# Half the drives of four sequences made by ScalarE and turned back by TensorE, and a rearranged head, in a fused scan and expert kernel

## The chip, the cores and the metric

One core of one Trainium2 chip runs the kernel. The metric is the device time of one execution in microseconds, and lower is better. The profile of one execution gives its span, from the first to the last instruction, and beside it that execution's own device time, which is a little longer than the span.

## What is computed

Eight sequences of 512 rows by 128 channels go through a selective state scan and then a mixture of experts (top 2 of 8). Cut to what matters here:

```python
xn = layernorm(layernorm(x)) * gamma + beta
dt = softplus(xn @ W_dt.T + b_dt)            # [T, D]
B, C = xn @ W_B.T, xn @ W_C.T                # [T, 16]
for n in range(16):                          # per state, per channel d
    h[t] = exp(-dt[t]*exp(A_log[d, n])) * h[t-1] + dt[t] * xn[t, d] * B[t, n]
    y[t] += C[t, n] * h[t]
x1 = x + layernorm(y + D * layernorm(x))
x2 = layernorm(x1);  gates = softmax(x2 @ gate_w + gate_b);  top 2 experts
out = x1 + layernorm(sum_k gate_k * (relu(x2 @ w1[e_k] + b1[e_k]) @ w2[e_k] + b2[e_k]))
```

All is float32. The product `dt * xn * B` is called the drive of a state, `exp(-dt*...)` its decay.

## The kernel before

In the scan part channels lie on partitions and time runs along the free dimension. Each sequence has 16 states, worked on in 8 pairs (`n` counts pairs over all sequences, `h` is the half). For one state VectorE makes the drive (`drive`, L915: `b_rep * gx_ps`, where `b_rep` is a row of B spread over all partitions by a DMA and `gx_ps = dt*xn` lies in PSUM) and then runs the scan (`scan`, L924). ScalarE makes the decay (`decay_`, L793). GpSimd multiplies both states of a pair with the spread C (`weigh`, L662), and TensorE sums them into `y_ps` by transposes (`reduce`, L1170). Two PSUM banks `u_ps[0]`, `u_ps[1]` hold the drives of the two halves (NU = 2), `hs` holds three pairs (NH = 3), and the decays have five buffers (NA = 5).

Ahead of each sequence's scans, ScalarE normalises (`norm`, L745), TensorE turns (L1136), ScalarE applies gamma and beta (`channels`, L767), TensorE makes B and C (`states`, L1151), ScalarE copies them (`rows`, L773) for a trip through DRAM, TensorE makes the logits of dt (`delta`, L1155), ScalarE makes the two halves of the softplus (L779 to L784), GpSimd adds them (`dt_add`, L653), and VectorE makes `gx_ps` (L904). All of these PSUM products share one bank, `misc`.

After every two sequences (a group) VectorE makes the routing, GpSimd scatters the 8 x 128 rows of the group twice by 16 indirect DMAs (L680) into expert slots in DRAM, and 23 tiles of 128 slots each go through `tile_turn`, `tile_up` (L1252, into `hid_ps`), `tile_relu` (ScalarE, L841, into `hid_t`), and `tile_down` (L1264). 92 tiles in all. The first banks and buffers of the tiles, `hid_ps` and `hid_t`, are idle until the first tile. At the end rows are gathered (L692), mixed on VectorE and stored.

Every engine works through one fixed list in order. The list is made in `planned()`, which plays the steps through a model: COST holds a modelled duration for each kind, `at(urgency, kind, ...)` names what a step waits for, and among the steps that are ready on an engine the smallest urgency number goes first. Where TensorE would idle, the planner puts a filler (`warm`, L1228), a bf16 matmul of zeros. SP alone issues the loads and stores, GpSimd the indirect ones.

The head of the program (before the list begins) loads sequence 0 and ten small parameters on SP, makes the statistics of sequence 0 on VectorE, waits on ScalarE for all ten small loads, exponentiates A_log there, waits for VectorE's sign change, and normalises sequence 0 on ScalarE.

## Time and profile before

| what | value |
|---|---|
| median of 3 runs | 479.35 us (477.76 to 479.82) |
| the profiled execution's own time | 477.24 us |
| its span | 475.5 us |
| busy of the span | PE 411.9 us (87%), DVE 354.3 (75%), ACT 317.7 (67%), POOL 297.5 (63%) |
| mean granted TensorE clock | 0.939 |

PE is TensorE (PEld its weight loads), DVE VectorE, ACT ScalarE, POOL GpSimd, SP SyncE. A busy PE in the scan part is to a large part fillers. The list of costliest groups is read by line; a stage table gives each engine's busy time within a stretch, which tells better than a share of the whole span which engine is full there.

### The profile page before, as it was taken

The numbers are of one execution on the slowest core, as the hardware profiler recorded it, in microseconds if no ns is written. First come the engines' busy times: TensorE is split into PE (matmuls) and PEld (weight loads), VectorE is DVE, ScalarE is ACT, GpSimd is POOL, SyncE is SP. The second block draws the span as 40 slices with busy tenths as digits, with TensorE's granted clock in tenths as the row PEclk, the third lists the DMA queues.
The fourth block names the chain that finished last, engine by engine and source line by source line (L and its number), as shares of the span: only waits on it lengthen the run. The fifth ranks groups of instructions, "written<-read, shape, count | busy, mean of one in ns | idle before, by whom it ended". The sixth has DMA issues, their size and how long they took to land.

```text
span 475.5 us, 9846 instructions
## 1 busy us (share of the span) xinstructions
PE 411.9 (87%) x2847; PEld 324.4 (68%) x2869; DVE 354.3 (75%) x834; ACT 317.7 (67%) x830; POOL 297.5 (63%) x219
## 2 busy tenths in 40 slices
PE   4459999998799989998989996699899999899950
PEld 1136566464456547897886796699799999899840
DVE  4699999999999999999999999596335524000355
ACT  3678584681377378779988867385775977667723
POOL 1157566481699946358995459578777770777720
PEclk8569999999899999999999999799999999899965
DMA  5699988896798878999899999984698788766341
GB/s 141 216 424 355 331 326 312 297 305 224 215 355 298 318 228 294 331 324 367 287 410 353 340 305 219 364 287 116 179 271 234 210 246 216 203 198 183 97 133 45
DMA packets 78147, 125.50 MB, mean 264 GB/s; under 512 B 7832, under 2 KB 50592, under 8 KB 74000
## 3 DMA queue, kind: packets, MB, share of 16 engines
q1 hardware_dynamic: 73776, 116.01, 75.2%
q0 software_dynamic: 4320, 8.86, 6.0%
q8 instruction: 26, 0.43, 0.4%
q14 instruction: 25, 0.20, 0.1%
HBM read 105.95 MB, written 18.89 MB: 263 GB/s over the span
## 4 chain that ended last, share of the span: by engine, by line
PE 30%; DVE 14%; DMA 8%; issue 7%; POOL 5%; ACT 5%; SPq 0%; DVEq 0%; ACTq 0%; POOLq 0%
PE out_ps L1264 10%; PE hid_ps L1252 7%; DMA w_tile<-w_rows 5%; DVE hs L924 4%; DVE u_ps L915 3%; POOL slots_in L680 3%; PE y_ps L1170 3%; ACT hid_t L841 3%; PE u_ps L1252 2%; DMA slots_in<-x,pos 2%; PE misc L1222 2%; POOL ch L662 1%; DMA xt<-slots_in 1%; ACT mix L860 1%; PE y_ps L1228 1%
## 5 line engine op out<-in xcount | busy, mean ns | idle before, releaser
L662 POOL TENSOR_TENSOR ch<-hs,c_rep 128x1024 f32<-128x1024 f32 x64 | 151.1, 2364 | 72.2 <-DVE hs L924 65.0
L924 DVE TENSOR_TENSOR_SCAN hs<-ab,u_ps 128x512 f32<-128x512 f32 x128 | 150.4, 1203 | 0.1
L793 ACT ACTIVATE ab<-dt,decay 128x512 f32<-128x512 f32 x128 | 89.3, 718 | 48.7 <-DVE hs L924 48.4
L1264 PE MATMUL out_ps<-w_f,hid_t 128*128 x736 | 102.8, 284 | 6.8 <-ACT hid_t L841 3.3
L1264 PEld LDWEIGHTS out_ps<-w_f,hid_t 128*128 128x128 f32 x736 | 91.6, 195 | 13.7 <-issue 12.0
L841 ACT ACTIVATE hid_t<-hid_ps,w_tile 128x128 f32<-128x128 f32 x244 | 69.2, 375 | 27.8 <-PE hid_ps L1252 20.0
L1228 PE MATMUL y_ps<-none 128*128 128x512 bf16 x351 | 85.9, 382 | 0.8
L915 DVE TENSOR_TENSOR u_ps<-b_rep,gx_ps 128x512 f32<-128x512 f32 x128 | 81.9, 678 | 0.2 <-issue 0.2
L680 POOL DMA_INDIRECT slots_in<-x,pos x64 | 64.7, 1012 | 25.8 <-issue 13.9
L1252 PE MATMUL hid_ps<-xt_t,w_tile 128*128 128x128 f32 x488 | 66.3, 280 | 9.1 <-DMA w_tile<-w_rows 6.5
L1170 PE MATMUL y_ps<-ident,ch 128*128 128x128 f32 x512 | 67.6, 277 | 5.8 <-POOL ch L662 5.8
L1170 PEld LDWEIGHTS y_ps<-ident,ch 128*128 128x128 f32 x512 | 59.2, 143 | 14.3 <-POOL ch L662 10.5
L1252 PEld LDWEIGHTS hid_ps<-xt_t,w_tile 128*128 128x128 f32 x488 | 60.3, 194 | 12.1 <-DMA w_tile<-w_rows 6.9
L1228 PEld LDWEIGHTS y_ps<-none 128*128 128x128 bf16 x371 | 36.4, 100 | 36.3 <-issue 3.3
L692 POOL DMA_INDIRECT c_rep<-slots_out,pos x32 | 31.7, 991 | 20.7 <-PE out_ps L1264 12.3
L1049 DVE SCALAR_TENSOR_TENSOR mix<-c_rep,weight,misc 128x128 f32<-128x128 f32 x24 | 6.7, 343 | 36.1 <-PE misc L1214 36.1
L841 ACT ACTIVATE hid_t<-u_ps,w_tile 128x128 f32<-128x128 f32 x84 | 24.0, 373 | 8.1 <-PE u_ps L1252 8.1
L850 ACT ACTIVATE ot<-out_ps 128x256 f32<-128x256 f32 (+1 forms) x48 | 18.3, 382 | 13.8 <-PE out_ps L1264 13.7
L703 POOL DMA_INDIRECT yg_dram<-ot,dst x23 | 22.7, 989 | 7.3 <-issue 7.3
L653 POOL TENSOR_TENSOR dt<-sp_l,sp_r 128x512 f32<-128x512 f32 x8 | 10.2, 1275 | 23.2 <-ACT sp_l L784 23.2
L1252 PE MATMUL u_ps<-xt_t,w_tile 128*128 128x128 f32 x168 | 22.4, 277 | 0.1
L1228 PE MATMUL out_ps<-none 128*128 128x512 bf16 x76 | 20.8, 408 | 1.3 <-DVE zeros L1095 1.3
(134 smaller groups left out, 482.1 us busy)
## 6 DMA issues: line engine op xcount, KB each, us to landing
b_rep<-rows_dram SPq DMA_DIRECT2D x64, 512.0 KB, 6.6
c_rep<-rows_dram SPq DMA_DIRECT2D x32, 1024.0 KB, 8.0
w_tile<-w_rows SPq DMA_DIRECT2D x92, 258.0 KB, 4.2
slots_in<-zeros SPq DMA_DIRECT2D x3, 1472.0 KB, 9.9
slots_out<-ot SPq DMA_DIRECT2D x33, 128.0 KB
xt<-slots_in SPq DMA_DIRECT2D x15, 256.0 KB
x<-x SPq DMA_DIRECT2D x8, 256.0 KB, 4.8
out<-mix SPq DMA_DIRECT2D x8, 256.0 KB, 2.5
```

Source lines behind the costliest of these rows:

```text
L662: nc.gpsimd.tensor_tensor(ch[:, n % NCH], hs[:, n % NH], c_rep[:, r // 2, 2 * (r % 2):2 * (r % 2) + 2].rearrange("p n t -> p (n t)"), ALU. ...
L680: nc.gpsimd.indirect_dma_start(out=slots_in[g], out_offset=bass.IndirectOffsetOnAxis(pos[:, r // K, K * b + r % K:K * b + r % K + 1], 0), ...
L692: nc.gpsimd.indirect_dma_start(out=yg(b)[:, r, :], out_offset=None, in_=slots_out[g], in_offset=bass.IndirectOffsetOnAxis(pos[:, r // K, K ...
L703: nc.gpsimd.indirect_dma_start(out=yg_dram, out_offset=bass.IndirectOffsetOnAxis(dst[:, i:i + 1], 0), in_=ot[:, m % NO, j * D:(j + 1) * D] ...
L793: nc.scalar.activation(ab[:, i % NA], dt[:, b % 2], ACT.Exp, scale=decay[:, 2 * r + h:2 * r + h + 1]).then_inc(s["decayed"], 1)
L841: last = nc.scalar.activation(hid_t[:, q % NHT, c * P:(c + 1) * P], hidden(q)[:, c * P:(c + 1) * P], ACT.Relu, bias=w_tile[:, q % NW, HID ...
L915: nc.vector.tensor_tensor(u_ps[i % NU][:], b_rep[:, n % NBR, h], gx_ps[:], ALU.mult).then_inc(s["driven"], 1)
L924: nc.vector.tensor_tensor_scan(hs[:, n % NH, h * T:(h + 1) * T], ab[:, i % NA], u_ps[i % NU][:], 0.0, ALU.mult, ALU.add).then_inc(s["scann ...
L1170: last = nc.tensor.matmul(y_ps[:, k * P:(k + 1) * P], ch[:, n % NCH, h * T + k * P:h * T + (k + 1) * P], ident[:], start=False, stop=(r == ...
L1228: nc.tensor.matmul(y_ps[:] if y_open else out_ps[:], none[:], none[:, 0:1].to_broadcast([P, T]), start=not y_open, stop=not y_open)
L1252: last = nc.tensor.matmul(hidden(q)[:, c * P:(c + 1) * P], w_tile[:, q % NW, c * P:(c + 1) * P], xt_t[:, m % NB, j * P:(j + 1) * P], start ...
L1264: last = nc.tensor.matmul(out_ps[:, j * D:(j + 1) * D], hid_t[:, q % NHT, c * P:(c + 1) * P], w2_f[:, bass.ds(e * HC * D + c * D, D)], sta ...
```

## The change

In sequences 0 to 3, in pairs 1 to 7 of each, the second half's drive (28 drives in all) is no longer made on VectorE from a spread row of B. Instead: once a sequence, TensorE makes B with time on partitions (`b_cols`, 4 small matmuls) and ScalarE copies it (`b_copy`); GpSimd makes a second `dt*xn` in SBUF (`gx_copy`); TensorE turns it into `hid_ps[1]` (`gx_turn`, 4 transposes). Once a drive, ScalarE multiplies the turned rows by the column of B as a per-partition scale, in four instructions of 128 x 128 (`weigh_gx`, into one of the three `hid_t` buffers), and TensorE turns the result back into `u_ps[1]` by 4 transposes (`u_turn`). For these pairs `b_spread` loads one row, not two. The tiles wait for the last `u_turn`, since they use the same buffers.

In the head, the parameters needed early come on two queues (two weights first on SP, five others on ScalarE's queue), the remaining three are loaded after the sequences; sequence 0 is normalised on VectorE, its delta goes to `hid_ps[0]` without waiting for the copy of the rows, and the sum of its softplus is made on VectorE right before `gx`. The fillers ahead of the first turn are 14, not 10, and two follow it; the planner places fillers from 16.0 us of its model, not 12.0, and starts each engine at a given time. Nearly all urgencies have new values, so that the lists of all engines are in another order to the end.

```diff
@@ constants and the planner @@
+TURNED_SEQS = 4
+TURNED = [b * PAIRS + r for b in range(TURNED_SEQS) for r in range(1, PAIRS)]
+TURN_NO = {n: j for j, n in enumerate(TURNED)}
+NSC = 3
-WARM, WARM_UP, HEAD_WARM = 0.26, 12.0, 10
+WARM, WARM_UP, HEAD_WARM, TURN_WARM = 0.26, 16.0, 14, 2
+BUSY_UNTIL = {"DVE": 6.1, "ACT": 6.4, "PE": 7.0, "POOL": 2.7, "SP": 8.5}
...
-    at(9.5, "weights_2", 0, 0, scan_of(2 * PAIRS))
+    at(1.5, "weights_2", 0, 0, scan_of(2 * PAIRS))
...
-        at(2.5, "stats", b, 0)
+        at(7.5, "stats", b, 0)
...
-        at(0, "gx", b, 0, ("dt_add", b, 0), ("drive", n0 - 1, 1))
+        at(12, "gx", b, 0, dt_of(b), last_drive(n0 - 1))
+        if b < TURNED_SEQS:
+            at(1.5, "b_cols", b, 0, ("channels", b, 0))
+            at(3.5, "b_copy", b, 0, ("b_cols", b, 0), ("weigh_gx", n0 - 1, 1))
+            at(14, "gx_copy", b, 0, dt_of(b), ("gx_turn", b - 1, 0))
+            at(2.5, "gx_turn", b, 0, ("gx_copy", b, 0), ("weigh_gx", n0 - 1, 1))
...
-            at(20, "spread", b, q, ("rows_out", b, 0), ("weigh", n0 - PAIRS + 2 * q + 1, 0))
+            at(10.5, "spread", b, q, ("rows_out", b, 0), ("weigh", n0 - PAIRS + 2 * q + 1, 0))
...
-                at(16.5, "drive", n, h, ("b_spread", n, 0), ("gx", b, 0), ("scan", *before(n, h, NU)))
+                if h and n in TURN_NO:
+                    j = TURN_NO[n]
+                    at(6.5, "weigh_gx", n, h, ("gx_turn", b, 0), ("b_copy", b, 0), *([("u_turn", TURNED[j - NSC], 1)] if j >= NSC else []))
+                    at(4.5, "u_turn", n, h, ("weigh_gx", n, 1), ("scan", *before(n, h, NU)))
+                else:
+                    at(21, "drive", n, h, ("b_spread", n, 0), ("gx", b, 0), ("scan", *before(n, h, NU)))
...
-            at(11.5, "weigh", n, 0, ("scan", n, 1), ("spread", b, n % PAIRS // 2), ("reduce", n - NCH, 0))
-            at(2, "reduce", n, 0, ("weigh", n, 0), ("skip_copy", b, 0), ("x1", b - 1, 0))
+            at(10, "weigh", n, 0, ("scan", n, 1), ("spread", b, n % PAIRS // 2), ("reduce", n - NCH, 0))
+            at(0.5, "reduce", n, 0, ("weigh", n, 0), ("skip_copy", b, 0), ("x1", b - 1, 0))
...
-                at(2, "scatter", b, r, ("slots", g, 0), ("clear", g, 0), *([("id_shift", b, 0)] if g == SENT and r >= K else []))
+                at(9, "scatter", b, r, ("slots", g, 0), ("clear", g, 0), *([("id_shift", b, 0)] if g == SENT and r >= K else []))
...
-            at(9, "tile_weights", q, 0, ("slots", g, 0), ("tile_relu", q - NW, 0))
+            at(0, "tile_weights", q, 0, ("slots", g, 0), ("tile_relu", q - NW, 0))
@@ SP @@
-                             rows_dram[b % 2][2 * r:2 * r + 2, :].rearrange("n t -> (n t)")[None, :]
-                             .to_broadcast([P, 2 * T])).then_inc(b_loaded[n % NBR], 16)
+                             rows_dram[b % 2][2 * r:2 * r + m, :].rearrange("n t -> (n t)")[None, :]
+                             .to_broadcast([P, m * T])).then_inc(b_loaded[n % NBR], 16)
...
+            for dst, src in ((w_bc[:], w_bc_t), (w_dt[:], w_dt_t)):
+                sp.dma_start(dst, src).then_inc(s["small_w"], 16)
@@ GpSimd @@
+            def gx_copy(b, _):
+
+                pool.wait_ge(s["dt_ready"], b + 1)
+                after(pool, s["gx_turned"], b)
+                nc.gpsimd.tensor_tensor(gx_s[:], dt[:, b % 2], xa[:, b % 2], ALU.mult).then_inc(s["gx_copied"], 1)
@@ ScalarE @@
+            def weigh_gx(n, h):
+
+                b, r = n // PAIRS, n % PAIRS
+                j = TURN_NO[n]
+                act.wait_ge(s["gx_turned"], b + 1)
+                act.wait_ge(s["b_copied"], b + 1)
+                after(act, s["u_turned"], j - NSC + 1)
+                for k in range(K):
+                    last = nc.scalar.activation(hid_t[:, j % NSC, k * P:(k + 1) * P], hid_ps[1][:, k * P:(k + 1) * P], ACT.Identity,
+                                                scale=b_t[:, k, 2 * r + h:2 * r + h + 1])
+                last.then_inc(s["u_weighed"], 1)
...
+            for dst, src in ((gam[:], gamma[:, None]), (bet[:], beta[:, None]), (decay[:], a_log), (bdt[:], b_dt[:, None]),
+                             (skip[:], d_param[:, None])):
+                act.dma_start(dst, src).then_inc(s["small_a"], 16)
             act.wait_ge(s["dve_set"], 1)
             scales(0, 1, 1)
-            act.wait_ge(s["small"], 16 * 10)
+            act.wait_ge(s["small_a"], 16 * 5)
@@ VectorE @@
             def gx(b, _):
 
+                if b == 0:
+                    dve.wait_ge(s["sp_log"], 1)
+                    nc.vector.tensor_tensor(dt[:, 0], sp_l[:], sp_r[:], ALU.add).then_inc(s["dt_ready"], 1)
                 dve.wait_ge(s["dt_ready"], b + 1)
...
-                dve.wait_ge(s["driven"], i + 1)
+                if h and n in TURN_NO:
+                    dve.wait_ge(s["u_turned"], TURN_NO[n] + 1)
+                else:
+                    dve.wait_ge(s["driven"], drives(n, h))
...
+            for k in range(K):
+                last = nc.vector.tensor_scalar(xn[:, 0, k], x1[:, k], rs[:, 1, 0, k:k + 1], nb_x[:, 1, 0, k:k + 1], ALU.mult, ALU.add)
+            last.then_inc(s["normed"], 1)
@@ TensorE @@
+            def b_cols(b, _):
+
+                pe.wait_ge(s["xa_ready"], b + 1)
+                misc_free("b_cols", b + 1)
+                for k in range(K):
+                    last = nc.tensor.matmul(misc[:, k * N:(k + 1) * N], xa[:, b % 2, k * P:(k + 1) * P], w_bc[:, 0:N], start=True,
+                                            stop=True)
+                last.then_inc(s["b_cols"], 1)
+
...
+            def u_turn(n, h):
+
+                j, i = TURN_NO[n], 2 * n + h
+                pe.wait_ge(s["u_weighed"], j + 1)
+                after(pe, s["scanned"], i - NU + 1)
+                for k in range(K):
+                    last = nc.tensor.matmul(u_ps[i % NU][:, k * P:(k + 1) * P], hid_t[:, j % NSC, k * P:(k + 1) * P], ident[:],
+                                            start=True, stop=True, is_transpose=True)
+                last.then_inc(s["u_turned"], 1)
```

## Rows read from the trace of the kernel before

**Rows 1.** The page: busy time of each engine, and 40 slices of the span.

```profile
PE 411.9 (87%) x2847; PEld 324.4 (68%) x2869; DVE 354.3 (75%) x834; ACT 317.7 (67%) x830; POOL 297.5 (63%) x219
...
DVE  4699999999999999999999999596335524000355
...
PEclk8569999999899999999999999799999999899965
```

**Rows 2.** Busy time by stage: from:to, length, then busy us of each engine.

```profile
21.30:48.90 27.60, 21.16 (x111) 13.44 (x114) 27.27 (x35) 21.02 (x40) 17.46 (x9) 0.80 0.99 389
48.90:81.70 32.80, 32.54 (x186) 19.40 (x187) 31.80 (x58) 21.34 (x40) 20.05 (x10) 1.00 0.91 319
81.70:126.50 44.80, 40.71 (x223) 22.76 (x226) 43.48 (x93) 23.15 (x44) 22.14 (x13) 1.00 0.78 263
126.50:160.50 34.00, 32.43 (x176) 19.54 (x180) 33.75 (x56) 21.45 (x41) 31.38 (x22) 0.95 0.95 326
...
390.00:455.00 65.00, 60.46 (x487) 56.97 (x487) 11.73 (x50) 43.93 (x147) 41.26 (x42) 0.97 0.64 176
```

**Rows 3.** Costliest groups: line, tiles, count, busy us and mean ns, idle before.

```profile
L662 POOL TENSOR_TENSOR ch<-hs,c_rep 128x1024 f32<-128x1024 f32 x64 | 151.1, 2364 | 72.2 <-DVE hs L924 65.0
L924 DVE TENSOR_TENSOR_SCAN hs<-ab,u_ps 128x512 f32<-128x512 f32 x128 | 150.4, 1203 | 0.1
...
L915 DVE TENSOR_TENSOR u_ps<-b_rep,gx_ps 128x512 f32<-128x512 f32 x128 | 81.9, 678 | 0.2 <-issue 0.2
...
L653 POOL TENSOR_TENSOR dt<-sp_l,sp_r 128x512 f32<-128x512 f32 x8 | 10.2, 1275 | 23.2 <-ACT sp_l L784 23.2
```

**Rows 4.** Timeline of VectorE in sequence 2: start us, duration us.

```profile
97.38 1.27 DVE L915 TENSOR_TENSOR u_ps<-b_rep,gx_ps 128x512 f32<-128x512 f32 x2
98.55 2.33 DVE L924 TENSOR_TENSOR_SCAN hs<-ab,u_ps 128x512 f32<-128x512 f32 x2
```

**Rows 5.** Timeline of the head, ScalarE and VectorE.

```profile
5.92 0.23 DVE L896 SCALAR_TENSOR_TENSOR nb_x<-mv,rs 128x4 f32<-128x4 f32 x2 [0.95 <-ACT rs L737]
...
8.46 0.21 ACT L868 ACTIVATE decay<-decay 128x16 f32<-128x16 f32 x1 [2.57 <-DMA gate_bias<-gate_b]
...
9.42 0.87 DVE L881 BATCH_NORM_STATS2 st<-x 128x6 f32<-128x128 f32 x4
...
17.35 0.38 DVE L885 BATCH_NORM_AGGREGATE mv<-st 128x2 f32<-128x6 f32 x4
21.34 0.70 DVE L904 TENSOR_TENSOR gx_ps<-dt,xa 128x512 f32<-128x512 f32 x1 [3.61 <-POOL dt L653]
...
23.73 2.32 DVE L924 TENSOR_TENSOR_SCAN hs<-ab,u_ps 128x512 f32<-128x512 f32 x2
```

**Rows 6.** Timeline of ScalarE: four 128-wide instructions from PSUM, and from SBUF.

```profile
284.29 1.15 ACT L841 ACTIVATE hid_t<-hid_ps,w_tile 128x128 f32<-128x128 f32 x4 [0.59 <-PE hid_ps L1252]
285.31 1.35 ACT L793 ACTIVATE ab<-dt,decay 128x512 f32<-128x512 f32 x2
```

```profile
8.92 1.65 ACT L745 ACTIVATE xn<-x,nb_x,rs 128x128 f32<-128x128 f32 x4 [0.24 <-DVE decay L1102]
```

**Rows 7.** TensorE: its granted clock by stretch (busy, then PEclk), and its timeline.

```profile
8.00:24.00 16.00, 6.16 (x12) 0.51 0.77 242
...
36.00:60.00 24.00, 23.75 (x138) 1.00 0.99 340
```

```profile
41.31 0.60 PE L1144 MATMUL misc<-ident,xu 128*128 128x128 f32 x4
...
42.39 1.03 PE L1170 MATMUL y_ps<-ident,ch 128*128 128x128 f32 x8
```

```profile
127.71 1.90 PE L1170 MATMUL y_ps<-ident,ch 128*128 128x128 f32 x8 [2.95 <-POOL ch L662]
```

**Rows 8.** The last scatter of group 0, and a stall of the tile stage.

```profile
162.86 1.27 POOL L680 DMA_INDIRECT slots_in<-x,pos  x1 [0.17 <-issue]
```

```profile
300.95 2.07 PE L1252 MATMUL hid_ps<-xt_t,w_tile 128*128 128x128 f32 x8 [5.68 <-DMA w_tile<-w_rows]
```

More of the change, by code:

```diff
@@ L104 @@
 HOP = 0.18
[L105 removed]
+WARM, WARM_UP, HEAD_WARM, TURN_WARM = 0.26, 16.0, 14, 2
+BUSY_UNTIL = {"DVE": 6.1, "ACT": 6.4, "PE": 7.0, "POOL": 2.7, "SP": 8.5}
 ROW_DMA, ROW_GAP = ("scatter", "gather", "tile_send"), 1.3
 ON = {
[L108 to L109 removed]
+    "DVE": "norm_first dt_first stats shift_all gx drive scan y_stats x1 x1_shift gate_bias gate_max softmax second starts slots mix mix_shift add tile_ids id_shift",
+    "ACT": "scales_all norm norm_u skip_copy channels rows softplus decay y_scale x1_scale x2 weigh_gx b_copy gate_copy gate_exp weigh_copy "
            "mix_scale result tile_copy tile_relu tile_keep",
[L111 to L112 removed]
+    "PE": "turn turn_u states b_cols gx_turn u_turn delta delta_first reduce gate_turn gate_logits count weigh_turn bias_mix tile_turn tile_pick tile_up tile_down",
+    "POOL": "gx_copy dt_add weigh scatter gather tile_send",
     "SP": "weights_2 clear rows_out b_spread spread tile_weights tile_load tile_store yg_load store",
@@ L149, in tasks @@
[L149 to L154 removed]
+        if b:
+            at(11, "norm", b, 0, ("shift_all", 0, 0), due)
+        else:
+            at(5, "norm_first", 0, 0)
@@ L510, in hidden, with drives @@
             return free[(q - alone) % len(free)]
+        def drives(n, h):
+            return 2 * n + h + 1 - sum(m < n or m == n and h == 1 for m in TURNED)
         def walk(parts):
@@ L1272, in _ @@
             turn_x(0, 0)
-            pe.wait_ge(s["small"], 16 * 10)
-            walk(dict(turn=lambda b, r: turn_x(b, r) if b else None, turn_u=turn_u, states=states, delta=delta, reduce=reduce,
+            for i in range(TURN_WARM):
+                warm(i, 0)
+            pe.wait_ge(s["small_w"], 16 * 2)
+            walk(dict(turn=lambda b, r: turn_x(b, r) if b else None, delta_first=delta, turn_u=turn_u, states=states, b_cols=b_cols, gx_turn=gx_turn, u_turn=u_turn, delta=delta, reduce=reduce,
                       gate_turn=gate_turn, gate_logits=gate_logits, count=count, weigh_turn=weigh_turn, bias_mix=bias_mix,
```

220 lines of the change are left out of this document (125 added, 95 removed).

## The prediction

> **What bounds the kernel now.** I read the page's slices first, then a table of busy time by stage, then the groups, and last the timelines of the head and of two spots. The slices [rows 1] show VectorE at nine tenths or more from the third slice to the twenty-fifth, so from about 24 to 297 us, while TensorE's 87% of busy time is partly fillers there. The stage table [rows 2] cuts the part that the change touches into the four sequences 0 to 3, from one `gx` to the next: 27.6 + 32.8 + 44.8 + 34.0 = 139.2 us, in which VectorE is busy 27.27 + 31.80 + 43.48 + 33.75 = 136.3 us (98%), ScalarE 87.0 and GpSimd 91.0. So VectorE sets the pace there, and nothing but its own list does. In the last of the four GpSimd is nearly as full, 31.38 of 34.0 us, since the 16 scatters of group 0 lie between its products. Behind the scans it is TensorE: 60.5 of 65 us busy in 390 to 455 [rows 2], with tiles, not fillers.
>
> **The drives taken from VectorE.** A drive lasts 678 ns and a scan 1203 ns in the groups [rows 3], but they overlap a little when queued. Two drives start at 97.38 and what follows starts at 98.55 [rows 4], so a drive costs 1.17 / 2 = 0.59 us of VectorE's time. 28 x 0.59 = 16.5 us leave it, 4.1 a sequence. That is the most the turned drives can give: 119.8 us of work in place of 136.3.
>
> **What ScalarE gets.** A turned drive is four 128-wide instructions that read PSUM with a per-partition operand. The nearest row is the tiles' relu, also four from PSUM: start 284.29, next instruction 285.31, so 1.02 us [rows 6]. The other bound is the normalisation, four from SBUF with two such operands, 1.65 us [rows 6]. I take 1.02, because the source is PSUM. The Trainium skill ("VectorE: DVE Perf Modes", section on the errata of SBUF sources) gives ScalarE 172 cycles plus one an element for PSUM and 224 for SBUF, at 1.2 GHz; an estimate by it is 4 x 0.25 = 1.0 us, and no run here shows the cause of the difference. Seven a sequence and one copy of B (at most the 0.26 us of one of the four): 7.4 us, or 11.8 at the other bound. Over four sequences ScalarE goes from 87.0 to 116.6 us, against VectorE's 119.8. By stage it is tighter. Some of its busy time is overlap that closes when it is full (a lone decay shows 0.72, a queued one 1.35 / 2 = 0.68, and the second of the relu group starts every 0.26 us while each lasts 0.38), some 1.5 us a sequence:
> - sequence 0: VectorE 27.27 - 4.1 = 23.2, ScalarE 21.0 + 7.4 - 1.5 = 26.9, of 27.6: ScalarE bounds, gain 0.7, with the fifth of it that it can put off to the next, 1.0.
> - sequence 1: VectorE 27.7, ScalarE 27.2, of 32.8: both full in lists that wait on each other, so 1 us above the larger and 0.5 for what was put off: gain 3.6.
> - sequence 2 has group 0's routing on VectorE: 39.4 against ScalarE 29.1, of 44.8: gain 4.1, the whole of it.
> - sequence 3: VectorE 29.6, ScalarE 27.4, GpSimd 31.4 + 1.3 for `gx_copy` (priced as the other 128x512 sum, 1275 ns [rows 3]) = 32.7, of 34.0. GpSimd bounds, but `hs` lets it lag three pairs into sequence 4: gain 2.0.
> Sum 10.7 us of the 16.5. The low bound is ScalarE at 1.65 us a drive: 11.8 + 21.3 - 1.5 = 31.6 us in each of sequences 0, 1 and 3, that is 0 (or 4 lost in sequence 0), 1 and 2 gained, 4 in sequence 2: some 3 us in all. The high bound is 16.5.
>
> **What TensorE gets.** 28 `u_turn`, 4 `gx_turn`, 4 `b_cols`, each four instructions: a turn of four is 0.60 us at the full clock [rows 7], so 21.6 us, in place of fillers, which fill far more than that. Price nothing while the fillers are the cover. On the path there is a deadline: `u_turn` of a pair can start only when the scan before it has freed `u_ps[1]`, and VectorE reaches the scan that needs it after one drive and one scan, 0.59 + 1.12 = 1.71 us. 0.60 us and two hops fit. Behind a `reduce` of 1.03 us [rows 7] it is 1.63 plus the hops, about late. Queued behind a late `u_turn` on VectorE are that scan, the next drives and through them GpSimd's product.
>
> **What leaves the DMA queues.** 28 rows less of B, 256 KB each: 7 MB. No engine waits for them: VectorE idled 0.2 us in all in front of its drives [rows 3]. So nothing.
>
> **The head.** Before, `nb_x` is there at 6.15, but ScalarE waits until 8.46 for the last of ten small loads, passes through the sign change, and normalises at 8.92 for 1.65 us [rows 5, 6]; TensorE's clock has then fallen to 1.2 GHz (0.51 granted from 8 to 24 us [rows 7]). `gx` starts at 21.34, the first scan at 23.73. After, the chain (normalise on VectorE at 6.2, turn 0.6, channels 0.8, states and delta 1.0 each at 2.4 GHz, softplus 2.6, hops) is done by about 14.3. But the sum for dt is written inside `gx`, and in the planner's list `gx` comes after the seven statistics (urgency 7.5 against 12). So VectorE's own list sets it: 6.15 + 1.1 to normalise (bounds 0.5 and 1.65) + 0.9 of small casts + the seven statistics, 17.73 - 9.42 = 8.3 us [rows 5] = 16.4; dt sum 0.7, `gx` 0.7, shift 0.3 (a broadcast row of B, asked for at about 12, must have landed by then), two drives 1.2: the first scan at 19.3, so 4.4 us earlier. Bounds: 3 us, if the five loads issued by ScalarE delay it or `gx` and GpSimd's `gx_copy` get in each other's way, and 6.5, if the statistics are spread out.
>
> **What follows.** From 160.5 us on the change removes nothing; it only comes earlier. Group 0's last scatter is at 162.86 [rows 8], so the tiles begin after the turned sequences in any case, and their wait for the last `u_turn` costs nothing. Tiles, scans, routing and mixing all hang on the scans before them, and TensorE has no free stretch behind them that would hold back the gain. So the whole 10.7 + 4.4 = 15.1 us arrives at the end. The new order from there on I price at nothing, bounds 5 us to both sides: before, it has a stall of 5.7 us for expert weights at 295 to 301 [rows 8], which could go or come twice. 477.24 - 15.1 = 462.1 against the profiled execution's own time; the median of the runs is 2.1 us above that, so 462 to 464, and I say 463.
>
> **Rivals.**
> - Full gain: ScalarE's work is spread well by the new urgencies, 16.5 + 4.4, perhaps with the stall gone: 451 to 456. For it: over four sequences all three engines fit below 120 us. Against: in-order lists, and sequence 0.
> - ScalarE is the bound: 1.3 us or more a drive, or its list stops in front of `weigh_gx` and holds the decays. Gain 3 + 4.4 down to 3: 470 to 476. For it: 26.9 of 27.6 us already at the low price.
> - The clock falls: in the turned sequences float32 transposes take the place of bf16 fillers. At 1.2 GHz a `reduce` is 1.90 us [rows 7] and a turn 1.1; 8 x 1.9 + 7 x 1.1 + some 9 us of the rest = 32 us a sequence, so TensorE would bound at 32 and only 4.4 + 5 remain: 468 to 470. Against: from 36 to 60 us such transposes stand among fillers and the clock granted is 1.00 [rows 7], and most fillers stay. The Trainium skill ("TensorE: Matmul & The Clock Gate", section on transposes) says that a transpose does not count as busy for the clock; by that rule this is the way it goes.
> - Slower: the turned drive comes late. One mechanism: `u_turn` stands behind a `reduce` in TensorE's list, which itself waits for GpSimd's product, and the scan behind it waits. If that is 1.3 us for each of the 28 (cold `reduce` 1.90 and turn 1.1 against the 1.71 there are), 36 us are lost: 477 - 15 + 36 = 498. It decides from 15.1 / 28 = 0.54 us a drive; at 1 us a drive the time is 490.
> - The drives leave, but nothing gains: head only and a worse order behind, 477 to 481.
>
> **Numbers.** Forecast 0.50 (456 to 469), full gain 0.17, ScalarE bound 0.12, clock 0.06, nothing 0.05, slower 0.10. A difference under 0.5%, 2.4 us, is what a measurement of this kernel cannot tell from none. Faster are the first four, 0.85; same 0.05; slower 0.10. The range 452 to 475 leaves out the slower cases, the edge of no gain and the best end.
>
> **What would show it.** In the stage table after, from one `gx` to the next: VectorE 4 us less busy in each of the four, ScalarE 7 more, at 95% or more in sequences 0 and 1. First scan at about 19.3, the statistics still in front of `gx`. Four `weigh_gx` instructions at 1.0 us. `gx` of sequence 4 at about 145.4 where it was at 160.5. VectorE's scans waiting for `u_turn` under 5 us in all. Wrong would be: VectorE idle for more than 15 us in that part, a granted clock under 0.9 from 40 to 140 us, or a tile stage longer than before by as much as the scans gained.

## The result and the profile after

The kernel after takes 486.15 us (median of 4 runs, 485.24 to 488.15), the kernel before beside it on the same chip 479.59 us: ratio 1.0151, 95% interval 1.0109 to 1.0192. The change makes the kernel 1.5% slower, where 463.0 us had been forecast. The profiled execution took 485.79 us, its span is 484.1 us.

The page of the kernel after, busy time and slices, against [rows 1]:

```profile
PE 423.4 (87%) x2964; PEld 341.1 (70%) x2991; DVE 351.8 (73%) x811; ACT 344.4 (71%) x942; POOL 302.0 (62%) x222
...
DVE  6878989999998999999999899487334534000255
...
PEclk9799999999899999999998979799999999999965
```

ScalarE has 27 us more work, as it should. VectorE has 2.5 us less, where 28 drives less at 678 ns each come to 19 us in the sum of durations, and the head's new work on it (normalisation and the dt sum) to 1.8 us more. So something gave VectorE time back. The mean granted clock is 0.947, before 0.939.

The stage table, the same four stretches as in [rows 2], from `gx` to `gx`, and sequence 4 and the tiles (length, then busy time of PE, PEld, DVE, ACT, POOL, granted clock):

```profile
17.38:48.30 30.92, 30.36 (x171) 19.02 (x174) 25.43 (x29) 25.61 (x65) 19.54 (x10) 0.91 0.60 218
48.30:82.50 34.20, 31.29 (x199) 21.13 (x202) 30.94 (x50) 28.16 (x70) 21.75 (x11) 1.00 0.67 241
82.50:129.80 47.30, 40.21 (x228) 25.42 (x231) 44.94 (x83) 33.34 (x85) 23.78 (x12) 0.93 0.79 277
129.80:160.30 30.50, 30.01 (x185) 19.39 (x187) 28.36 (x50) 26.20 (x61) 27.75 (x20) 1.00 0.82 283
160.30:204.30 44.00, 41.16 (x280) 30.23 (x283) 42.81 (x84) 29.19 (x68) 28.05 (x15) 1.00 0.88 294
390.00:455.00 65.00, 62.53 (x516) 58.52 (x516) 13.73 (x62) 45.49 (x152) 38.63 (x40) 1.00 0.71 194
```

The head is 4 us shorter, about as forecast: `gx` of sequence 0 starts at 17.38, not 21.34. But the four turned sequences take 142.9 us in place of 139.2, so `gx` of sequence 4 comes at 160.3, where it came before (160.5), and not at 145.4. In the new list 62 scans stand ahead of that `gx`, before 63, so for like work (a scan is 1.1 us) the part is nearer 4.8 us longer. VectorE's busy time in them went from 136.3 to 129.7 us, not to 119.8, and its idle time from 2.9 to 13.2. ScalarE is nowhere near full (25.6 of 30.9), and neither is GpSimd, which in sequence 3 is at 27.75 of 30.5. Behind sequence 4's `gx`, where no code changed, the kernel after takes 484.1 - 160.3 = 323.8 us against 315.0 before: 8.8 us more, of which 7.7 are in the scans (they end at 337.3, before at 329.8). So the result splits in three: head -4.0, turned part +3.7, behind it +8.8, together +8.5, where the spans differ by 8.6.

What VectorE waits for in the turned part, as the waits of the trace list them (us in total, times, longest):

```profile
DVE hs L998 <- PE u_ps L1264: 5.8, 9, 1.3
DVE nb_x L963 <- ACT rs L778: 1.5, 1, 1.5
DVE gx_ps L975 <- POOL dt L688: 1.3, 2, 0.7
DVE hs L998 <- issue: 0.5, 1, 0.5
```

That is 9 of the 13.2 us of idle time; the others are short gaps, such as the 0.09 us between the end of a lone drive and its scan. The rest of the loss hides inside instructions. The timeline of VectorE at a pair with one drive, and at `gx` of sequence 1, then GpSimd at that place:

```profile
75.58 0.67 DVE L986 TENSOR_TENSOR u_ps<-b_rep,gx_ps 128x512 f32<-128x512 f32 x1
76.34 2.42 DVE L998 TENSOR_TENSOR_SCAN hs<-ab,u_ps 128x512 f32<-128x512 f32 x2
78.67 0.68 DVE L986 TENSOR_TENSOR u_ps<-b_rep,gx_ps 128x512 f32<-128x512 f32 x1
...
48.30 2.83 DVE L975 TENSOR_TENSOR gx_ps<-dt,xa 128x512 f32<-128x512 f32 x1 [0.66 <-POOL dt L688]
```

```profile
48.22 2.35 POOL L703 TENSOR_TENSOR ch<-hs,c_rep 128x1024 f32<-128x1024 f32 x1
50.53 1.72 POOL L694 TENSOR_TENSOR gx_s<-dt,xa 128x512 f32<-128x512 f32 x1
```

Two things are to be read here. First, the pair lasts 78.67 - 75.58 = 3.09 us (3.01 to 3.10 in the others that wait for nothing). In the kernel before, a pair with two drives starts at 97.38 [rows 4], and the next row of that timeline is

```profile
100.79 1.27 DVE L915 TENSOR_TENSOR u_ps<-b_rep,gx_ps 128x512 f32<-128x512 f32 x2
```

so that pair lasts 3.41 us (3.42 in most). The first scan starts 0.76 us after the lone drive, where two drives together took 1.17: the scan reads what the drive before it has just written, and nothing stands between them. So a drive that leaves is worth 1.17 - 0.76 = 0.41 us, and 0.33 to 0.41 by the whole pair, not 0.59. Second, `gx` lasts 2.83 us where [rows 5] has 0.70. It isn't shown as waiting, but it ends 0.56 us after GpSimd's product does (48.22 + 2.35 = 50.57; 48.30 + 2.83 = 51.13), and `gx_copy`, which GpSimd starts at 50.53, takes 1.72 us in place of 1.27. Both engines seem to take turns.

### The profile page after: what moved, and what is told of

Same layout as the page of the kernel before. It is cut to its first block, busy times and chain, and to the rows that moved or that the text cites. A ratio compares the mean times of both kernels' runs of the same rounds, so it can differ in the third digit from the quotient of the medians.

```text
span 484.1 us, 10253 instructions
## 1 busy us (share of the span) xinstructions
PE 423.4 (87%) x2964; PEld 341.1 (70%) x2991; DVE 351.8 (73%) x811; ACT 344.4 (71%) x942; POOL 302.0 (62%) x222
## 4 chain that ended last, share of the span: by engine, by line
PE 31%; DMA 8%; issue 7%; POOL 5%; ACT 4%; DVE 4%; SPq 1%; POOLq 0%; ACTq 0%; DVEq 0%
PE out_ps L1377 11%; PE hid_ps L1365 7%; PE u_ps L1365 3%; DMA w_tile<-w_rows 2%; PE misc L1335 2%; ACT hid_t L906 2%; PE y_ps L1281 2%; PE gx_ps L1365 2%; POOL ch L703 1%; DMA slots_out<-ot 1%; POOL slots_in L721 1%; DMA slots_in<-x,pos 1%; PE misc L1327 1%; DMA rows_dram<-rows 1%; POOL yg_dram L744 1%
## 5 line engine op out<-in xcount | busy, mean ns | idle before, releaser
L1377 PEld LDWEIGHTS out_ps<-w_f,hid_t 128*128 128x128 f32 x736 | 91.2, 195 | 14.5 <-issue 13.0
L1365 PE MATMUL hid_ps<-xt_t,w_tile 128*128 128x128 f32 x488 | 69.0, 287 | 6.7 <-issue 5.3
L1341 PE MATMUL y_ps<-none 128*128 128x512 bf16 x268 | 70.0, 385 | 1.1 <-issue 0.2
L1365 PEld LDWEIGHTS hid_ps<-xt_t,w_tile 128*128 128x128 f32 x488 | 62.9, 201 | 8.7 <-issue 8.3
L986 DVE TENSOR_TENSOR u_ps<-b_rep,gx_ps 128x512 f32<-128x512 f32 x100 | 65.0, 680 | 0.6 <-issue 0.3
L1341 PEld LDWEIGHTS y_ps<-none 128*128 128x128 bf16 x292 | 29.0, 100 | 25.4 <-issue 4.2
L843 ACT ACTIVATE hid_t<-hid_ps,b_t 128x128 f32<-128x128 f32 x112 | 31.4, 386 | 5.5 <-PE hid_ps L1254 3.4
L1341 PE MATMUL out_ps<-none 128*128 128x512 bf16 x116 | 32.2, 422 | 1.4 <-DVE zeros L1171 1.3
L906 ACT ACTIVATE hid_t<-u_ps,w_tile 128x128 f32<-128x128 f32 x84 | 24.0, 372 | 11.4 <-PE u_ps L1365 11.2
L733 POOL DMA_INDIRECT yg_first<-slots_out,pos x16 | 15.4, 962 | 14.2 <-DMA slots_out<-ot 9.9
L1341 PEld LDWEIGHTS out_ps<-none 128*128 128x128 bf16 x119 | 12.6, 107 | 15.8 <-issue 6.0
```

The source lines that it names most:

```text
L733: nc.gpsimd.indirect_dma_start(out=yg(b)[:, r, :], out_offset=None, in_=slots_out[g], in_offset=bass.IndirectOffsetOnAxis(pos[:, r // K, K ...
L843: last = nc.scalar.activation(hid_t[:, j % NSC, k * P:(k + 1) * P], hid_ps[1][:, k * P:(k + 1) * P], ACT.Identity, scale=b_t[:, k, 2 * r + ...
L906: last = nc.scalar.activation(hid_t[:, q % NHT, c * P:(c + 1) * P], hidden(q)[:, c * P:(c + 1) * P], ACT.Relu, bias=w_tile[:, q % NW, HID ...
L986: nc.vector.tensor_tensor(u_ps[i % NU][:], b_rep[:, n % NBR, h], gx_ps[:], ALU.mult).then_inc(s["driven"], 1)
L1341: nc.tensor.matmul(y_ps[:] if y_open else out_ps[:], none[:], none[:, 0:1].to_broadcast([P, T]), start=not y_open, stop=not y_open)
L1365: last = nc.tensor.matmul(hidden(q)[:, c * P:(c + 1) * P], w_tile[:, q % NW, c * P:(c + 1) * P], xt_t[:, m % NB, j * P:(j + 1) * P], start ...
```

## The experiments

The kernels up to undo_same_list ran on chips on which the kernel before itself takes 503 to 505 us, the others where it takes 479; each ratio is to the kernel before on the same chip. On a slower chip the kernel before has `gx` of sequence 4 at 160.9, as on the other (160.5), and its whole surplus lies behind the scans. So the times up to there can be read across both.

### Head, turned drives and new lists apart

**head_old_order**, **all_old_order** and **new_order_no_turn** let the planner make new lists, with the urgencies of before for the first two.

```diff
# head_old_order: the kernel after with
-TURNED_SEQS = 4
+TURNED_SEQS = 0
-        todo[kind, i, part] = (urgency,
+        todo[kind, i, part] = (OLD.get(kind, urgency),      # the urgencies of before
# all_old_order: the second edit alone; new_order_no_turn: the first alone
```

> The head of the change and all its other code, no turned sequence, and the urgencies of the kernel before. Both theories (A: the new order of the lists costs the time; B: the turned drives themselves cost it) expect the 4.0 us that gx came earlier in the changed kernel: 475.6 against a before of 479.6. If it is 478 or more, the 4 us of the head are given back later whatever the drives do.

> The whole change, but with the urgencies of the kernel before (new kinds keep theirs, norm_first, delta_first and dt_first take those of norm, delta and dt_add). Theory A (the new order costs the time): 462 to 470, gx of sequence 4 at 150 or earlier. Theory B (the turned drives cost it): 476 to 482, gx of sequence 4 near 160 as in the changed kernel.

> The changed kernel with no turned sequence, new urgencies and new head. Theory A: 482 to 488, as slow as the changed kernel or slower. Theory B: 472 to 477, the head's gain and nothing else.

Measured: 1.0316 (1.0239 to 1.0392), 1.0846 (1.0772 to 1.0919) and 1.0034 (0.999 to 1.0078). Old urgencies fit neither the new head (`gx` of sequence 0 at 26.1 us, later than before) nor the turned work (`gx` of sequence 4 at 176.2). Lists planned from urgencies that were chosen for another graph cost 3% with the new head alone, and 8% with the turned drives in them. So a kernel that is planned anew measures its lists first and its edit second.

new_order_no_turn fell between its two theories. It has `gx` of sequence 0 at 17.4, `gx` of sequence 4 at 158.2 and the end of the scans at 332.2. Two things follow. The new urgencies lose 5.3 us between `gx` of sequence 4 and the end of the scans (174.1 against 168.8 in before_again) with no turned drive in the kernel. And the kernel after is slower than the same urgencies without turned drives: 1.0151, and 1.0192 on a slower chip, against 1.0034 there. With the lists planned anew for each, the turned drives cost over 1%.

**drop28** leaves the 28 drives out of the kernel before and plans anew; the scans of these pairs read a product that is left over in their bank, so the output is another one.

> The kernel before with 28 drives left out (second halves of pairs 1 to 7 in sequences 0 to 3; their scans run over what the bank held, so the output is wrong), nothing in their place. It is the most that VectorE can be given. If a drive is worth 0.59 us, as predicted: 479.6 - 16.5 = 463. If the first drive's result is exposed once no second drive stands behind it (a pair took 3.02 to 3.09 us in the changed kernel, against 3.42), 28 x 0.37 = 10 us: 469. If the gain is lost behind the scans: 475 or more.

It took 1.0289 (1.0224 to 1.0354): less work on the fullest engine, and 2.9% slower. Its one profile (of an execution of 524.67 us, the median is 518.35) shows where: `gx` of sequence 4 comes at 152.9, so the four sequences take 131.6 us in place of 139.2, 1.1 us of it a scan that stands behind that `gx` here. Behind it all is lost again, since the scans end at 344.5 where they ended at 329.8, and VectorE waits there 7.4 us for `y_ps` and 7.0 us for `rs_y` from ScalarE. In other lists, then, a good half of the freed time does arrive at the end of this part. From here on lists were held fixed.

**before_again** and **after_again** are both kernels as they are.

> The kernel before, unchanged, for a trace on the chip of this call: the first four runs fell on a chip where it took 505 us, not 479. Both theories expect the ratio 1.00 to itself. It is to show in which stage and on which engine a chip's 25 us lie (if DMA: landing times up and waits for w_tile; if an engine: its mean durations up).

> The changed kernel, unchanged, beside the others of this call. If the 1.5% are the same on every chip: ratio 1.010 to 1.020. If they depend on how a fixed list meets a chip's transfer times, the ratio can be anything from 0.98 to 1.05.

The kernel before showed a span of 507.4 us there in its one profiled execution; the kernel after has ratio 1.0192 (1.0124 to 1.0261), in line with the first chip.

### The drives, with the lists held

**drop28_same_list** keeps every list of the kernel before and only skips 28 drives. **undo_same_list** keeps every list of the kernel after and puts the drives back on VectorE, each as early as its bank allows, with no turned work.

```diff
# drop28_same_list: the kernel before with
+DROP = [(8 * b + r, 1) for b in range(4) for r in range(1, 8)]
             def drive(n, h):
+                if (n, h) in DROP:
+                    return
# undo_same_list: the kernel after with
-b_cols=b_cols, gx_turn=gx_turn, u_turn=u_turn, b_copy=b_copy, weigh_gx=weigh_gx, gx_copy=gx_copy,
+# drive(m, 1) is issued right after drive(m, 0) and scan(m - 1, 1)
```

> The kernel before with the 28 drives left out (their scans run over what the bank held, so the output is wrong) and every list otherwise exactly as before; the first time the planner had made new lists for it, and it was 2.9% slower. Theory A (new lists cost the time, and a drive less is a drive less): ratio 0.965 to 0.98, that is 10 to 16 us less, from 0.37 to 0.59 us a drive. Theory B (VectorE's time in sequences 0 to 3 is not what the end hangs on): ratio 0.99 to 1.00.

> The changed kernel with its lists as they are, but the 28 drives back on VectorE, each behind the first drive of its pair, and nothing of the turned work issued (weigh_gx, u_turn, gx_copy, gx_turn, b_cols, b_copy), two rows of B loaded. Theory A (order): 3 to 10 us slower than the changed kernel, since VectorE gets 28 drives back in unchanged lists. Theory B (the turned work costs what it gives): within 3 us of the changed kernel or faster than it.

drop28_same_list: 0.9972 (0.9931 to 1.0013). From `gx` to `gx` over four sequences it takes 140.8 us, before 139.2 (139.4 on this chip), though 11.4 us of work left VectorE. This run breaks the forecast's main step, in the lists of before, without any turned work in it. Its VectorE groups in this stretch (busy and mean ns of one; the fifth `gx` is that of sequence 4), and the timelines of VectorE and of GpSimd around one of the small shifts of a normalisation:

```profile
L909 DVE TENSOR_TENSOR gx_ps<-dt,xa 128x512 f32<-128x512 f32 x5 | 10.7, 2131 | 3.6 <-POOL dt L658 3.6
L953 DVE SCALAR_TENSOR_TENSOR nb<-mv,rs 128x4 f32<-128x4 f32 x3 | 7.3, 2426 | 0.3 <-ACT rs L732 0.2
L942 DVE SCALAR_TENSOR_TENSOR shift<-mv_y,rs_y 128x4 f32<-128x4 f32 x3 | 2.8, 924 | 0.3 <-ACT rs_y L732 0.3
```

```profile
145.49 0.67 DVE L922 TENSOR_TENSOR u_ps<-b_rep,gx_ps 128x512 f32<-128x512 f32 x1
146.08 2.67 DVE L953 SCALAR_TENSOR_TENSOR nb<-mv,rs 128x4 f32<-128x4 f32 x1
148.67 1.21 DVE L931 TENSOR_TENSOR_SCAN hs<-ab,u_ps 128x512 f32<-128x512 f32 x1
```

```profile
145.36 0.98 POOL L685 DMA_INDIRECT slots_in<-x,pos  x1 [0.17 <-issue]
146.37 2.35 POOL L667 TENSOR_TENSOR ch<-hs,c_rep 128x1024 f32<-128x1024 f32 x1
```

An instruction on four columns takes 2.67 us and ends as GpSimd's product ends (148.75 and 148.72). In this part of this run all the lines that stretch so read two tensors from SBUF: `gx`, `nb`, `shift`, and in the routing `r_sub` and `run` (elsewhere `eq` and others). Scans and drives, which read one operand from PSUM, never do: none is over 1.22 and 0.70 us in any trace. But two inputs are not the whole condition. In the kernel after a cast with one input does the same, VectorE and then GpSimd:

```profile
126.05 1.89 DVE L1111 CAST pos<-pos_f 128x16 uint32<-128x16 f32 x1
```

```profile
125.44 2.46 POOL L703 TENSOR_TENSOR ch<-hs,c_rep 128x1024 f32<-128x1024 f32 x1 [6.01 <-DVE hs L998]
```

In the 17 traces 235 VectorE instructions last over 0.5 us more than their shortest, and each of them ends 0.01 to 0.57 us behind the end of a product or a sum on GpSimd, which is its own shortest time less 0.09 to 0.15 us: as if it began when GpSimd's ended. Counting for each such group what it takes over its shortest duration (0.70 us for `gx`, 0.15 for `nb` and `shift`, 0.22 to 0.29 for the routing's), the four sequences hold 6.3 us of it before, 18.0 in drop28_same_list, and 13.6 in the kernel after (1.7 of it the cast). Against the 11.4 us freed stand 11.7 us more of such waits. In the old rhythm of 3.42 us a pair these instructions met few products.

undo_same_list: 1.0345 (1.0274 to 1.0415), against 1.0192 for the kernel after in its own lists: 8.1 us slower with the drives put back. So in lists made for it the turned work beats the drives, 4.6 us of it in the turned part (147.7 from `gx` to `gx`, 143.0 in after_again). But no list was made for the drives put back here; where one was, in new_order_no_turn, the kernel without turned drives is the faster.

### Each half of the change in before's lists

In these the step lists of all engines were written into the kernel as they stand in the kernel before. **head_same_list** takes the new head alone. In **turned_same_list** each of the 28 drives leaves its list, its `weigh_gx` stands 5 us ahead on ScalarE's and its `u_turn` at its place on TensorE's. **after_then_before_list** follows the kernel after up to `gx` of sequence 4 and then the order of the kernel before.

```diff
 def order():
...
-    return planned(alone), alone
+    for item in LISTED.split(";"):       # LISTED: the steps written out, kind, i, part, time
+        kind, i, part, time = item.split()
+        steps.append((float(time), kind, int(i), int(part)))
+    return steps, 41
```

> The new head alone (two load queues, normalisation and dt sum of sequence 0 on VectorE, no turned drives) run through the exact written-out lists of the kernel before, where the planner has no say. Theory 'the head pays, new lists lose it': gx of sequence 0 near 17.4 us, 4 us earlier than before, all eight sequences shifted by 3 to 4 us, ratio 0.992 to 0.995. Rival 'an earlier head is lost again in the sequences that follow, whatever the lists' (waits of VectorE for GpSimd's products): gx of sequence 4 less than 1.5 us earlier than in before, ratio 0.998 to 1.003.

> The whole change (new head and 28 turned drives), but with the lists of the kernel before: each turned drive leaves VectorE's list, its weigh_gx stands 5 us ahead of that place on ScalarE and its u_turn at that place on TensorE. Theory 'freed VectorE time is eaten by waits for GpSimd's products, as where the drives were only left out': gx of sequence 0 near 17.4 us, gx of sequence 4 at best at 157 us, ratio 0.990 to 1.000. Rival 'the turned work is sound and only the replanned lists lost': gx of sequence 4 at 150 us or earlier, ratio 0.970 to 0.985. Rival 'turned work itself costs, by waits for u_turn': VectorE idle over 10 us for it in the four sequences, ratio above 1.01.

> The kernel after up to the start of gx of sequence 4 in its own lists, and from there on the order of the kernel before. Theory 'the 9 us behind gx of sequence 4 are the new lists alone': gx of sequence 4 at about 160 us as in both, and from there to the end as long as in before, ratio 0.998 to 1.003. Rival 'something the first four sequences leave behind (routing of group 0 done 7 us later, tiles started later) costs it, whatever the list behind': ratio 1.010 to 1.020.

head_same_list: 475.68 us, ratio 0.9932 (0.9909 to 0.9956), faster than both kernels. Its head on VectorE, then the last `gx` of the part:

```profile
17.70 0.70 DVE L1364 TENSOR_TENSOR gx_ps<-dt,xa 128x512 f32<-128x512 f32 x1
18.31 0.28 DVE L1352 SCALAR_TENSOR_TENSOR nb_x<-mv,rs 128x28 f32<-128x28 f32 x2
18.51 1.29 DVE L1375 TENSOR_TENSOR u_ps<-b_rep,gx_ps 128x512 f32<-128x512 f32 x2
19.71 2.33 DVE L1387 TENSOR_TENSOR_SCAN hs<-ab,u_ps 128x512 f32<-128x512 f32 x2
...
156.87 2.65 DVE L1364 TENSOR_TENSOR gx_ps<-dt,xa 128x512 f32<-128x512 f32 x1
```

156.87 - 17.70 = 139.2 us, to the tenth what the kernel before has. The head's gain is carried through four sequences, 3.7 us of it, and by the ratio 3.3 us arrive at the end.

turned_same_list: 490.64 us, 1.0246 (1.0216 to 1.0276); `gx` of sequence 4 at 174.2. VectorE waits 10.0 us for `u_turn`, 5.4 of it at once; the last rival in its expectation named that. It was one placing by hand and not the best one, so it does not show the least that the turned work must cost.

after_then_before_list: 483.08 us, 1.010 (1.0072 to 1.0128), between the two theories. Its stages, from `gx` of sequence 4 on:

```profile
161.20:210.00 48.80, 44.62 (x298) 32.96 (x299) 42.72 (x93) 32.10 (x76) 26.78 (x15) 0.97 0.84 277
210.00:243.00 33.00, 31.14 (x243) 27.04 (x242) 31.82 (x57) 30.52 (x81) 30.05 (x21) 1.00 0.95 333
243.00:290.40 47.40, 43.85 (x338) 37.48 (x337) 46.15 (x94) 38.38 (x102) 29.39 (x19) 1.00 0.96 346
290.40:334.00 43.60, 35.65 (x294) 34.54 (x294) 35.01 (x57) 27.24 (x81) 32.96 (x21) 0.92 0.90 252
```

The kernel before has 45.5, 33.0, 47.3 and 43.4 us there, the kernel after 44.0, 36.5, 50.1 and 46.4. With the old order the last three are those of before again. Of the 8.8 us behind `gx` of sequence 4 the order of before thus takes back 5.6 us, which agrees with the 5.3 us that new_order_no_turn loses there. 3.2 us (318.2 against 315.0) stay, all of it in sequence 4, where VectorE waits 4.8 us once for `y_ps` of sequence 3. On GpSimd's timeline six scatters of group 0 stand between 154.4 and 168.9 us, the last products of sequence 3 between and behind them; three of them (161.54, 163.12 and 164.40 us) stand in a row ahead of the last product but one, where the kernel after's own list alternates scatter and product. In its own order the kernel after takes only 44.0 us for sequence 4. So the 3.2 us may come of joining two orders at this place; that the first part leaves them behind whatever follows is not shown.

### Does VectorE wait for GpSimd's instruction to end?

**drop28_one_input** is drop28_same_list, but `gx` reads one tensor (the factor dt is left out), and the two shifts take `rs` as a per-partition operand, so that they read one tensor too.

```diff
-nc.vector.tensor_tensor(gx_ps[:], dt[:, b % 2], xa[:, b % 2], ALU.mult)
+nc.vector.tensor_scalar(gx_ps[:], xa[:, b % 2], 1.0, None, ALU.mult)
-nc.vector.scalar_tensor_tensor(out=nb_1[:], in0=mv_1[:, :, 0], scalar=-1.0, in1=rs_1[:], ...)
+for k in range(K):
+    nc.vector.tensor_scalar(nb_1[:, k:k + 1], mv_1[:, k, 0:1], rs_1[:, k:k + 1], -1.0, ALU.mult, ALU.mult)
```

> As the kernel with before's lists and 28 drives left out (ratio 0.997 there, and the sequences read stale products), but gx reads one tensor from SBUF (xa, the factor dt is left out), and the two small shifts are written as four instructions each with the rs as per-partition operand, so that they too read one tensor. Theory 'an instruction of VectorE with two SBUF tensors waits until GpSimd's running product is done, and this ate the 11 us': gx, nb and shift show under 0.8 us each time, gx of sequence 4 is reached 8 to 11 us earlier than with two inputs (130 to 133 us after gx of sequence 0, where it was 140.8), ratio 0.96 to 0.98. Rival 'they wait for something else, such as the data': gx and nb stay at 2 to 3 us in some sequences, ratio 0.995 to 1.000.

Ratio 0.9922 (0.9892 to 0.9952); 136.8 us from `gx` to `gx`, where 130 to 133 had been expected. The groups, and then VectorE's waits in this part:

```profile
L909 DVE TENSOR_SCALAR gx_ps<-xa 128x512 f32<-128x512 f32 x4 | 2.7, 679 | 3.5 <-POOL dt L658 3.5
L943 DVE TENSOR_SCALAR shift<-mv_y,rs_y 128x1 f32<-128x1 f32 x12 | 1.7, 201 | 0.3 <-ACT rs_y L732 0.3
L954 DVE TENSOR_SCALAR nb<-mv,rs 128x1 f32<-128x1 f32 x12 | 1.7, 201 | 0.0
```

```profile
DVE st_y L886 <- PE y_ps L1178: 6.0, 3, 3.3
DVE gx_ps L909 <- POOL dt L658: 3.5, 1, 3.5
DVE u_ps L922 <- DMA b_rep<-rows_dram: 2.7, 2, 1.4
DVE logit L961 <- PE misc L1194: 1.6, 3, 0.6
```

The stretching of these lines is gone, with the semaphore waits in front of them as they were: the theory on its cause holds. Its worth does not: VectorE is busy 122.6 us instead of 133.9, but idle 14.2 instead of 6.9. The longest new wait is for `y_ps`, the sum of the last pair; as I read it, its product on GpSimd and its `reduce` have a latency that VectorE's list used to cover. The new form has a price too: the 24 one-column instructions take 3.4 us, where the six they replace would take 0.9 unblocked. So of 11.4 us freed, 2.4 arrive (139.2 to 136.8), and they arrive at the end: span 473.2 against 475.5. Behind `gx` of sequence 4 the edit takes away some 10 us more of such waits, and from there to the end of the scans the kernel takes 169.4 us, where drop28_same_list takes 169.8. So most of these waits cover others: taken away, they are not gained.

**head_split_product**, **after_split_product** and **drop28_split_product** cut GpSimd's product in two halves and leave all else.

```diff
-nc.gpsimd.tensor_tensor(ch[:, n % NCH], hs[:, n % NH], c_rep[...], ALU.mult).then_inc(s["weighed"], 1)
+for h in range(2):
+    last = nc.gpsimd.tensor_tensor(ch[:, n % NCH, h * T:(h + 1) * T], hs[:, n % NH, h * T:(h + 1) * T],
+                                   c_rep[:, r // 2, 2 * (r % 2) + h], ALU.mult)
+last.then_inc(s["weighed"], 1)
```

> The new head in the lists of the kernel before (ratio 0.993 alone), and GpSimd's product of a pair of states, 128x1024 and 2.36 us, written as two instructions of 128x512, some 1.2 us each. Theory 'a VectorE instruction with two SBUF tensors waits for the end of GpSimd's running instruction': the longest gx, nb, run and r_sub fall from 2.4 to 3.4 us to at most 1.7 us, VectorE's busy time in the scans falls by 6 to 10 us, ratio to before 0.975 to 0.988. Rival 'the two share a port and slow each other by a share of their time, however the product is cut': these instructions stay at 2.4 us and more at the same places, ratio 0.990 to 0.997, or above 1.0 if the extra instruction slows GpSimd.

> The kernel after with its own lists and the product on GpSimd in two halves. Theory 'waits for the end of GpSimd's instruction': gx of sequences 1 and 2 falls from 2.83 to under 1.7 us, eq, pos_h, cand, hot and the cast of pos to under 1.5 us each, time 8 to 14 us under that of the kernel after, ratio to before 0.985 to 1.000. Rival 'the loss is in the waits for u_turn and in the order of the lists, not in this': under 3 us gained, ratio to before 1.008 to 1.015.

> 28 drives left out in the lists of the kernel before (those sequences read stale products), the product on GpSimd in two halves. Theory 'waits for the end of GpSimd's instruction': of the 11.4 us freed, which vanished with whole products (140.8 us from gx of sequence 0 to gx of sequence 4 against 139.2), some half arrive: 132 to 136 us; ratio to before 0.965 to 0.980. Rival: 139 us or more, ratio 0.990 to 1.000.

Ratios 0.9905 (0.9872 to 0.9937), 1.0208 (1.0147 to 1.0269) and 0.9977 (0.9953 to 1.0001). From `gx` to `gx` drop28_split_product takes 140.4 us, where 132 to 136 had been expected and 140.8 stood with whole products: its rival came out. VectorE in drop28_split_product, a shift that comes during a half, and one that comes during a scatter; then GpSimd at both:

```profile
93.76 1.22 DVE L954 SCALAR_TENSOR_TENSOR nb<-mv,rs 128x4 f32<-128x4 f32 x1 [0.15 <-ACT rs L733]
144.11 2.82 DVE L954 SCALAR_TENSOR_TENSOR nb<-mv,rs 128x4 f32<-128x4 f32 x1
```

```profile
93.69 2.50 POOL L668 TENSOR_TENSOR ch<-hs,c_rep 128x512 f32<-128x512 f32 x2 [4.10 <-DVE hs L932]
...
143.41 0.98 POOL L686 DMA_INDIRECT slots_in<-x,pos  x1 [0.17 <-issue]
144.42 2.49 POOL L668 TENSOR_TENSOR ch<-hs,c_rep 128x512 f32<-128x512 f32 x2
```

At 93.76 VectorE gets in after the first half (1.22 us, where whole products made it 2.30). At 144.11 it comes while the scatter's instruction runs, and waits through both halves (ends at 146.93, they at 146.91). The longest `gx` of head_split_product is the same case, 3.36 us at 155.96, over a scatter and both halves. In after_split_product `gx` of sequences 1 and 2 falls from 2.83 to 1.75 us. So the wait is for GpSimd's running product, in halves where it came during one, and the expected 1.7 us at most was wrong where it came during a scatter; why it isn't let in between the halves there is open. In sum the stretching of two-tensor instructions fell from 21.8 to 14.5 us (head), from 29.6 to 16.8 (after) and in the four sequences from 18.0 to some 13 (drop28). With it one-input instructions stretched that had not before: the routing's `cnt_i` (shortest 0.17 us) took 1.07 us three times in head_split_product and ended as a half did. The time fell by little or not at all. head_split_product, at 473.01 us the fastest kernel here, is not told apart from head_same_list (1.3 us by the ratios, and the intervals overlap). For the kernel after the rival came out right: taking away 13 us of waits did not make it faster. The test is not a clean one, since its waits for `u_turn` rose from 5.8 to 8.1 us and GpSimd's two halves take 2.5 us, the whole 2.36.

## Why the prediction was wrong, step by step

- **The head**: right up to `gx`, which starts at 17.38 (the forecast's terms give 17.1), statistics in front of it, 4.0 us earlier. The 4.4 us had been forecast for the first scan, and there the kernel's own lists gain 2.8: it came at 20.94, not 19.3, since `nb_x` waits 1.46 us for ScalarE. In before's lists it comes at 19.71, 4.0 us earlier, and most of that reaches the end.
- **"A drive costs 1.17 / 2 = 0.59 us of VectorE's time"**: wrong in size. 1.17 us is right for two together. Taking one away leaves a drive and a scan that depends on it with nothing between, and takes away 0.33 to 0.41. At 0.41 the 28 are 11.4 us, not 16.5.
- **"10.7 of 16.5 us arrive", and VectorE's busy time falling by 4 us a sequence**: this is the step that failed. The measured part is 3.7 us longer. The terms from the trace: -11.4 for the drives; +7.3 for instructions stretched behind GpSimd's (13.6 against 6.3); +5.8 for `u_turn`; +1.2 for `nb_x` (1.46 against 0.28); +1.3 for `gx` waiting for a late dt; +0.5 in front of scans; -0.9 for a wait for `y_ps` that is gone. The sum is +3.8, and good to about 1 us, for it leaves out the scan moved behind `gx` (-1.1) and prices every drive at the top of its range. The forecast took VectorE's busy time as work that stays the same when the rhythm changes, and it does not. That none of the freed time can arrive is not shown: with the drives left out and lists planned for that (drop28), some 6.5 us did by `gx` of sequence 4 (7.6 less the moved scan).
- **"ScalarE bounds" in sequences 0 and 1**: no. It was 83% and 82% busy. Its own prices held: four `weigh_gx` at 1.12 us (31.4 us of busy time in 28), and 26 us more in four sequences, 113.3 against 87.0. That is inside the forecast's 116.6.
- **"u_turn waits under 5 us"**: 5.8 us, longest 1.3; just above. The measured time lies where the rival "slower" put it, but its mechanism, late turns, is 5.8 us here and not the 15 or more that it needs. Nor does it explain the result alone: with the drives back on VectorE the same lists are 8.1 us slower still.
- **"The whole 15.1 us arrives at the end"** and **"the new order from there on I price at nothing, bounds 5 us"**: the second failed. It cost some 5.5 us: of the 8.8 us lost behind `gx` of sequence 4 the old order takes back 5.6, and new_order_no_turn loses 5.3 there. The other 3.2 us are open. The first stands where it could be tried: what was gained at `gx` of sequence 4 in head_same_list (3.7) and in drop28_one_input (2.4) is at the end 2.5 and 2.3 us.
- **The clock**: the granted clock in the turned sequences is 0.91, 1.00, 0.93 and 1.00 in the mean, though transposes took the place of fillers there. It falls to 0.50, the 1.2 GHz level, in two places: from 16 to 22 us (0.52 in the mean), after TensorE did nothing from 14 to 16, and from 120 to 124 us, after it had waited 3.3 us for `mask` of the routing. Before, it fell at the routing too (0.59 from 128 to 132 us). The rival "the clock falls", which had all four sequences at 1.2 GHz, is out. The Trainium skill ("TensorE: Matmul & The Clock Gate", section on transposes) says that a transpose does not count as busy for the clock; here 62 to 84 fillers a sequence stand among them, so this case doesn't test that rule alone.

What stays open: how far the two-tensor waits and the new lists could be tuned away together. The wait in the kernel after is shown to exist and its cause is shown by the one-input and half-product runs, but removing half of it did not shorten that kernel, so its 7.3 us are a term of the account and not a proven loss. Why the turned work costs over 1% against new_order_no_turn, when both are planned, is shown by no single run. Which of the new urgencies cost the 5.6 us behind sequence 4 was not tried.

## What to carry to other kernels

When work leaves the fullest engine, price it by what the engine's next instruction then waits for: look for a stretch where the neighbour stands alone, and ask which waits are hidden by what leaves. Busy time is not fixed work where VectorE and GpSimd run at once: compare mean with shortest duration by group; a mean of several times the shortest was here a wait in disguise. But a wait that is found is not yet time that can be had: take it away and measure, for another wait may stand behind it. And if lists come from a planner, try an edit in the old lists, written out, before judging it by new ones: here the head, the half of the change that pays, is 0.7% faster by itself in the old lists, where the whole with new lists was 1.5% slower.
